# One ring of PSUM banks, late low parts on GpSimd and a new table of slots in a fused attention kernel

## The reference, cut to what matters

```python
xn = _layernorm(x)                                   # x: (8, 1024, 512), f32
out = x + attention(xn, ...) + ffn(xn, ...)

# attention: 16 heads of 64, two null keys and values for each head
a = layernorm(xn) * norm_g + norm_b
q = l2norm((a @ Wq).heads) * q_scale
k, v = split(xn @ Wkv);  k = l2norm([null_k, k]) * k_scale;  v = [null_v, v]
sim = q @ k.T * 8 + slopes[h] * -|j - i|             # ALiBi bias
sim = where(causal, sim, -max)
o = softmax(sim) @ v;  attention = o.reshape(...) @ Wout
```

## Time and profile before

| | us |
|---|---|
| median of 3 runs | 2699.43 |
| lowest, highest | 2696.95, 2702.16 |
| the profiled execution, its own time | 2701.09 |
| its span in the profile | 2699.3 |
| TensorE busy | 2627.6 (97%) |
| TensorE weight load busy | 1578.7 (58%) |
| VectorE busy | 2483.1 (92%) |
| ScalarE busy | 2127.0 (79%) |
| GpSimd busy | 2103.5 (78%) |

### The profile page before, as it was taken

How to read it: one execution, slowest core, us unless ns; L and a number is a source line. 1 busy time by engine, 2 the same in 40 slices (tenths; PEclk the granted TensorE clock), 3 DMA queues, 4 the chain that set the end, 5 groups by cost and what they waited for, 6 DMA issues and landing times.

```text
span 2699.3 us, 84329 instructions
## 1 busy us (share of the span) xinstructions
PE 2627.6 (97%) x31631; PEld 1578.7 (58%) x31631; DVE 2483.1 (92%) x6756; ACT 2127.0 (79%) x3385; POOL 2103.5 (78%) x2442
## 2 busy tenths in 40 slices
PE   5899999999999999999999999999999999999997
PEld 4456556565565565565565565566555665565654
DVE  8999998999989999999999999999999999989996
ACT  5688887888877888877888878788887888877876
POOL 6677887779867788678877788778887778877774
PEclk7899999999999999999999999999999999999999
DMA  5333354334544344433443436443453434544222
GB/s 170 74 67 72 79 105 98 89 73 82 100 100 94 69 87 97 98 85 78 96 103 82 89 75 102 102 92 72 78 106 89 101 71 78 100 102 74 57 56 71
DMA packets 638789, 236.94 MB, mean 88 GB/s; under 512 B 594608, under 2 KB 596656, under 8 KB 638384
## 3 DMA queue, kind: packets, MB, share of 16 engines
q1 hardware_dynamic: 636912, 231.45, 40.4%
q10 hardware_dynamic: 1472, 0.09, 0.0%
HBM read 72.01 MB, written 16.78 MB: 33 GB/s over the span
## 4 chain that ended last, share of the span: by engine, by line
PE 84%; DVE 7%; DMA 3%; issue 3%; POOL 2%; SPq 1%; ACT 1%; ACTq 0%; POOLq 0%; DVEq 0%
PE PS L1268 13%; PE PS L1245 12%; PE PS L1246 11%; PE PS L1247 11%; PE PS L1292 6%; PE PS L1331 6%; PE PS L1335 4%; PE PS L1333 4%; PE PS L1272 4%; PE PS L1358 4%; PE PS L1359 4%; PE PS L1360 4%; DVE PS L1044 2%; PE PS L1303 1%; DVE QKB L1064 1%
## 5 line engine op out<-in xcount | busy, mean ns | idle before, releaser
L1044 DVE CUSTOM_DVE_ANT_0 PS<-PS,STR 128x512 f32<-128x512 f32 (+3 forms) x1536 | 822.5, 580 | 124.3 <-PE PS L1292 117.4
L598 ACT ACTIVATE AR<-PS,SC 128x1024 f32<-128x1024 f32 (+1 forms) x640 | 655.0, 1023 | 146.5 <-PE PS L1303 76.8
L1245 PE MATMUL PS<-WH,XT 128*128 128x388 f16 x2048 | 677.3, 331 | 20.7 <-DVE AR L1057 10.8
L1246 PE MATMUL PS<-WL,XT 128*128 128x388 f16 x2048 | 674.6, 329 | 0.0
L1247 PE MATMUL PS<-WH,XT 128*128 128x388 f16 x2048 | 674.2, 329 | 0.0
L602 ACT ACTIVATE AR<-AR 128x1024 f16<-128x1024 f32 (+1 forms) x640 | 621.7, 971 | 20.3
L810 POOL TENSOR_TENSOR RN<-SS,HALF 128x8 f32<-128x8 f32 x256 | 453.6, 1772 | 179.2 <-DVE SS L1132 178.0
L1085 DVE TENSOR_TENSOR AR<-AR 128x768 f16<-128x768 f32 (+1 forms) x448 | 503.1, 1134 | 13.2 <-ACT AR L602 13.2
L1268 PE MATMUL PS<-AR 64*128 64x512 f16 (+3 forms) x4608 | 496.7, 324 | 9.2 <-ACT AR L598 9.2
L1331 PE MATMUL PS<-AR 128*128 128x66 f16 x4608 | 473.0, 195 | 2.1 <-DVE AR L1085 1.2
L1333 PE MATMUL PS<-AR 128*128 128x64 f16 x4608 | 469.4, 192 | 0.0
(11 more groups left out here) (227 smaller groups left out, 5199.7 us busy)
## 6 DMA issues: line engine op xcount, KB each, us to landing
XW<-in_L_attn_x SPq DMA_DIRECT2D x112, 256.0 KB, 3.1
XB<-in_L_attn_x SPq DMA_DIRECT2D x64, 256.0 KB, 2.9
out<-ACC SPq DMA_DIRECT2D x64, 256.0 KB, 2.3
ACC<-in_L_attn_x SPq DMA_DIRECT2D x56, 256.0 KB, 3.0
AR<-QKB SPq DMA_TRANSPOSE x512, 2.5
AR<-in_L_attn_Wkv SPq DMA_DIRECT2D x2, 1536.0 KB, 12.7
ACC<-in_L_attn_x SPq DMA_DIRECT2D x2, 1024.0 KB, 7.1
AR<-in_L_attn_Wout SPq DMA_DIRECT2D x1, 2048.0 KB, 8.3
```

The costliest lines, as they stand in the source:

```text
L598: e.activation(PR[:, n % 2, :, 0:wide], SB[:, :, 0:wide], ACT.Exp, scale=SIG).then_inc(s_p, 1)
L1044: e.tensor_tensor_reduce(out=r[:, 0:n], in0=r[:, 0:n], in1=ST[:, u % 2, h, o:o + n], scale=1.0, scalar=LOW, op0=ALU.add, op1=ALU.max, accu ...
L1245: e.matmul(to, XT[:, k, xs], WH[:, k, p, :], start=k == 0, stop=False)
L1246: e.matmul(to, XT[:, k, xs], WL[:, k, p, :], start=False, stop=False)
```

## The change

- **One ring of six banks** (0 to 5) now serves scores, pieces, projected and output tiles. A score step takes two adjacent banks (`take_pair`), and `bank_free` waits for the exp that read them last. AV moves to banks 6 and 7. TensorE issues pieces ahead of scores in a slot.
- **Pieces in groups**: the 12 pieces become 10 groups; (0,0) and (2,0) share a pair of banks, and so do (4,1) and (6,1). Matmuls and maxima are the same in number and size.
- **The cast** of a step (L602) has a slot of its own, `W_CAST`, and no longer follows its exp directly.
- **Late low parts** 8 to 15 are made by GpSimd in two instructions each, a scaling in place and a difference (`W_LATP`, semaphores s_spr and s_spq). The transposes of unit 1 and the projections of unit 2 wait for them.
- **The maxima** of the weights are turned in bank 5, without the wait for s_bqe; those of Wout in bank 6.
- The wait for s_nv2 ahead of the value matmuls goes (the null step stands ahead on the same engine).
- **New slots**: 50 to a unit and new offsets in all tables, of which the diff shows some.

```diff
-BANKS = 4
-SL = 48
+BANKS = 6
+SL = 50
-PIECES = [(qt, c) for qt in range(NT) for c in range(1 + qt // 4)]
+GROUPS = [[(0, 0), (2, 0)], [(3, 0)], [(1, 0)], [(4, 0)], [(5, 0)], [(4, 1), (6, 1)], [(6, 0)], [(5, 1)], [(7, 0)], [(7, 1)]]
...
-W_PIECE = [47, 53, 56, 59, 66, 68, 69, 77, 79, 82, 83, 86]
-W_MAX = [41, 45, 49, 55, 64, 64, 66, 72, 75, 75, 76, 84]
-W_SCORE = [88, 96, 105, 108, 111, 115, 118, 126, 130, 133]
-W_OTS = [109, 149]
-W_OP = [121, 121, 138, 149, 160, 160, 167, 170]
...
+W_PIECE = [56, 56, 63, 68, 78, 88, 88, 89, 92, 94]
+W_MAX = [57, 58, 62, 73, 79, 85, 85, 87, 95, 98]
+W_SCORE = [97, 98, 110, 111, 115, 115, 120, 128, 140, 141]
+W_CAST = [99, 102, 111, 111, 115, 116, 122, 129, 142, 142]
+W_OTS = [118, 155]
+W_OP = [141, 145, 145, 151, 171, 191, 194, 207]
...
-W_STAT = [-288, -194, -181, -174, -128, -113, -101, -96]
-W_XF = [-73, -53, -29, -6, -6, 11, 18, 20]
+W_STAT = [-335, -285, -235, -222, -209, -200, -167, -161]
+W_XF = [-111, -87, -60, -20, -6, 4, 12, 28]
...
-HOLD = [2.0, 2.1, 2.0, 6.7]
+HOLD = [9.6, 10.6, 11.8, 12.7, 10.3]
...
-W_LATD = [-313, -246, -231, -193, -187, -179, -171, -128, -96, -89, -73, -68, -67, 17, 19, 20]
-W_XL0 = [-78, -1]
-W_WOM = [30, 40, 41]
-W_WOT = [46, 53]
+W_LATD = [-376, -343, -342, -342, -314, -290, -252, -192]
+W_LATP = [-218, -169, -149, -144, -79, -78, -57, 48]
+W_XL0 = [0, 26]
+W_WOM = [-159, -11, 11]
+W_WOT = [25, 37]
...
+def pieces(g):
+    out, at = [], 0
+    done = 2 * sum(len(z) for z in GROUPS[:g])
+    for qt, c in GROUPS[g]:
+        n = min(512, P * (qt + 1) - 512 * c)
+        out.append((qt, c, at, n, done))
+        at += n
+        done += 2
+    return out
 
...
+    def take_pair(slot, u, m):
+        i = min(range(BANKS - 1), key=lambda z: (max(read[z], read[z + 1]), read[z] + read[z + 1]))
+        for h in range(2):
+            who = ("sc", u, 2 * m + h)
+            at[who], before[who] = i + h, last[i + h]
+            last[i + h], read[i + h] = who, slot
...
+        for u, m in due(s, W_SCORE):
+            take_pair(s + HOLD[4], u, m)
...
-        SB, AV = PS[:, 0:2, :], PS[:, 2:4, 0:264]
+        AV = PS[:, 6:8, 0:264]
...
-            return PS[:, 4 + BANK[who], :]
+            return PS[:, BANK[who], :]
...
-                e.wait_ge(s_mx, 24 * u + i + 1)
+                e.wait_ge(s_mx, 24 * u + pieces(i // 2)[-1][4] + i % 2 + 1)
+            elif what == "sc":
+                e.wait_ge(s_p, NS * u + i // 2 + 1)
...
-                        w.wait_ge(s_spl, 24)
+                        w.wait_ge(s_spq, 4)
...
+                    low = BANK["sc", u, 2 * m]
                     w.wait_ge(s_st, 2 * n + 2)
                     w.wait_ge(s_wo, 8)
                     pl_done(w, n - 2)
-                    e.activation(PR[:, n % 2, :, 0:wide], SB[:, :, 0:wide], ACT.Exp, scale=SIG).then_inc(s_p, 1)
+                    e.activation(PR[:, n % 2, :, 0:wide], PS[:, low:low + 2, 0:wide], ACT.Exp, scale=SIG).then_inc(s_p, 1)
+                for u, m in due(s, W_CAST):
+                    n = NS * u + m
+                    wide = width(m)
                     w.wait_ge(s_p, n + 1)
...
+                for _, i in due(s, W_LATP, 1, BL):
+                    src, scale, hi, lo = late(8 + i)
+                    w.wait_ge(s_wact, 12 + 8 + i + 1)
+                    e.tensor_scalar(src, src, scale, None, ALU.mult).then_inc(s_spr, 1)
+                    w.wait_ge(s_spr, i + 1)
+                    e.tensor_tensor(lo, src, hi, ALU.subtract).then_inc(s_spq, 1)
...
-                    qt, c = PIECES[i]
-                    n = min(512, P * (qt + 1) - 512 * c)
-                    o = 896 - P * qt + 512 * c
-                    w.wait_ge(s_s, 24 * u + 2 * i + 2)
-                    w.wait_ge(s_str, 2 * u + 2)
-                    if u:
-                        w.wait_ge(s_m, 3 * (2 * (u - 1) + qt // 4) + 3)
-                    for h in range(2):
-                        r = rb("s", u, 2 * i + h)
-                        e.tensor_tensor_reduce(out=r[:, 0:n], in0=r[:, 0:n], in1=ST[:, u % 2, h, o:o + n], scale=1.0, scalar=LOW,
-                                               op0=ALU.add, op1=ALU.max,
-                                               accum_out=MX[:, qt // 4, qt % 4, h, c:c + 1]).then_inc(s_mx, 1)
+                    for qt, c, at, n, done in pieces(i):
+                        o = 896 - P * qt + 512 * c
+                        w.wait_ge(s_s, 24 * u + pieces(i)[-1][4] + 2)
+                        w.wait_ge(s_str, 2 * u + 2)
+                        if u:
+                            w.wait_ge(s_m, 3 * (2 * (u - 1) + qt // 4) + 3)
+                        for h in range(2):
+                            r = rb("s", u, 2 * i + h)
+                            e.tensor_tensor_reduce(out=r[:, at:at + n], in0=r[:, at:at + n], in1=ST[:, u % 2, h, o:o + n], scale=1.0,
+                                                   scalar=LOW, op0=ALU.add, op1=ALU.max,
+                                                   accum_out=MX[:, qt // 4, qt % 4, h, c:c + 1]).then_inc(s_mx, 1)
                 for u, t in due(s, W_VL):
...
-            w.wait_ge(s_bqe, 3)
-            e.transpose(PS[0:8, 2, 192:320], AM[:, 0:8], IDF[:, :]).then_inc(s_amt, 1)
+            e.transpose(PS[0:8, 5, 0:128], AM[:, 0:8], IDF[:, :]).then_inc(s_amt, 1)
...
-                        w.wait_ge(s_spl, 28)
+                        w.wait_ge(s_spl, 20)
+                        w.wait_ge(s_spq, 8)
...
+                for _, i in due(s, W_WOT, 1, BL):
+                    if i == 0:
+                        w.wait_ge(s_wo, 1)
+                        e.transpose(PS[0:1, 6, 0:P], AM[:, 5:6], IDF[:, :]).then_inc(s_won, 1)
+                    else:
+                        w.wait_ge(s_wop, 1)
+                        e.matmul(PS[:, 6, P:P + 1], ONE[0:1, :], M8[0:1, :], start=True, stop=True).then_inc(s_won, 1)
+                for u, i in due(s, W_PIECE):
+                    bank_free(w, "s", u, 2 * i)
+                    bank_free(w, "s", u, 2 * i + 1)
+                    for qt, c, at, n, done in pieces(i):
+                        for g in range(qt // 2 + 1):
+                            w.wait_ge(s_kq[g], 32 * (u + 1))
+                        for h in range(2):
+                            hs = slice(64 * h, 64 * h + 64)
+                            e.matmul(rb("s", u, 2 * i + h)[:, at:at + n], KQ[hs, u % 2, QH, P * qt:P * qt + P],
+                                     KQ[hs, u % 2, KH, 512 * c:512 * c + n], start=not at, stop=True,
+                                     skip_group_check=True).then_inc(s_s, 1)
                 for u, m in due(s, W_SCORE):
                     qc, blocks = STEPS[m]
-                    n = NS * u + m
-                    w.wait_ge(s_p, n)
+                    low = BANK["sc", u, 2 * m]
+                    bank_free(w, "sc", u, 2 * m)
+                    bank_free(w, "sc", u, 2 * m + 1)
                     for g in range(max(2 * qc + 1, blocks[-1][0] // 2) + 1):
                         w.wait_ge(s_kq[g], 32 * (u + 1))
                     w.wait_ge(s_ct[qc], 16 * (u + 1))
...
-                                e.matmul(SB[:, h, to], KQ[hs, u % 2, a, ks], KQ[hs, u % 2, c, qs],
+                                e.matmul(PS[:, low + h, to], KQ[hs, u % 2, a, ks], KQ[hs, u % 2, c, qs],
...
-                    if blocks[0][0] == 0:
-                        w.wait_ge(s_nv2, 2 * u + qc + 1)
```

127 lines of the change are left out of this document (55 added, 72 removed).

## The result

| | before | after |
|---|---|---|
| median, us | 2699.27 (2696.95 to 2702.16, 4 runs) | 2714.62 (2714.09 to 2718.99, 4 runs) |
| ratio, 95% interval | | 1.0065 (1.0053 to 1.0077) |
| span of the profiled execution | 2699.3 | 2712.3 |

The change costs 15 us; 2689 was forecast. The 13.0 us between the two profiled spans lie as follows (before, from the first projection of units 0, 4 and 63, as in the earlier trace rows): to the first projection 47.80 and now 45.75; units 0 to 3 147.84 and now 156.96, +9.1; units 4 to 62 2393.94 and now 2398.25, +4.3; the end 109.7 and now 111.3, +1.6. So I read the start from unit 0's first projection on.

What follows compares the result with a forecast made beforehand. TensorE's own work was taken as the floor, busy 2382.89 of the middle's 2394.0 us. Switches -1.2, maxima -0.6, start +4, middle -8, end -5 sum to -10.8 from 2699.4: 2689 us, range 2674 to 2711 (8 in 10).

Steps and rivals of the forecast that it cites:

- The middle: Units 4 to 62: ring and new slots give back half of the 16.3 us lost, 8 us; bounds 0 and 16.3.
- the bunching: VectorE's layer-norm work crowding some units of the middle; claimed milder after the change, the reason for the 8 us gain.
- The double waits: Matmul with two semaphore waits behind a short null step: 0.16 us lost once a unit, stays; 0 taken, bounds 6.4 either way.
- The start: Before the steady units: VectorE idles for Wout's load, GpSimd's low parts stay hidden; 4 us lost, bounds 0 and 8.
- The end: Behind the last units: score matmuls wait less for exp, 5 of 7.8 us gained; bounds 7.8 gain, 3 loss.
- Switches and maxima bank: TensorE: 12 fewer switches between 128-row and 64-row matmuls, 1.2 us less; start: maxima in their own bank, 0.6 less.
- Rival 1: Second null step waits for VectorE to read the accumulator AV: 16 us slower than forecast, 2705 us; chance 0.18.
- Quiet unit: Sign in the middle: period of a unit without layer norm stays 40.3 us within 0.1.
- Batch boundaries: Sign in the middle: units at batch boundaries take 41.4 us at most, not 42.2.

Runs made afterwards that it cites:

- e4_ott: Changed kernel with the first transfer that transposes attention outputs (OT<-OTK) at slot 125 instead of 129 in SyncE's order; 2698.25 us.
- e6_waits: e4_ott with two more waits of TensorE, on semaphores already reached, ahead of each of 640 score steps; 2697.59 us.
- e3_both: Changed kernel with Wout's maximum back behind the first evictions and late low parts 8 to 15 on VectorE again; 2714.02 us.
- e14_start: e7_start_ott with the steps of Wout's maximum later, VectorE's first at slot 38 instead of 31; 2694.24 us.
- e7_start_ott: e5_start with the transfer OT<-OTK at slot 125; 2694.30 us.
- e13_null: e4_ott with the wait for s_nv2, the end of TensorE's own null step, put back ahead of each half's first value step; 2710.52 us.
- e5_start: Changed kernel with all orders of once-only steps from the kernel before, Wout's maximum scaled to the new unit; 2715.07 us.
- e10_wot: e7_start_ott with TensorE's steps for Wout's maximum at slots 60 and 75, VectorE's second and third and the casts behind them; 2697.69 us.
- e2_lows: Changed kernel with late low parts 8 to 15 made by VectorE again, none by GpSimd; 2713.69 us.

## Why the prediction was wrong

**The middle (-8 in the sum; +4.3 measured).** This step failed, and it decided the sign. Its argument was that the ring and the new slots "can give back" at most 16.3 us and cost nothing, so its lower bound was 0. Taken apart by `e4_ott` there are two terms: -15.9 for ring, pieces and orders, and +20.2 for the transfer of OT, which the prediction never priced. That -15.9 lies near the bound of 16.3 is luck: 9.5 of it are the waits of the next paragraph, which sat in every quiet unit and so outside the 16.3. What is left for the bunching, 6.4, is near the 8 that were taken, though one of the two reasons given was misread: of a batch's eight L938 at most five lay within 48 slots before, not six. For the transfer, the prediction had the table: W_OTT moved from 109 to 129, W_OP from 121 to 141, the same distance of 20, and W_TP of the unit two ahead stands at 125, now ahead of the transfer, with loads of x behind it in two units of eight. A moved step was counted on TensorE, VectorE and GpSimd, and not on the queue that issues its transfer.

**The double waits (0, "the 0.16 stays").** Wrong in cause. They were waits for the ring, 9.5 us in 58 units, and went. Two more waits ahead of each score step cost nothing (`e6_waits`). The clue was in the trace: a gap that is named "issue" and is the same everywhere.

**The start (+4; +9.1 for units 0 to 3, +7.1 for the time at which unit 4 begins).** Right in its first mechanism, the wait for Wout, but too small; its upper bound of 8 held for the 7.1 and not for the 9.1. VectorE idled 7.91 us (8 forecast), the first eviction came at 74.40 (77.2 forecast), unit 3's first projection at 162.1, 6.7 late and not 4. GpSimd's low parts were called hidden and weren't: seven of them took 18.8 us and stood ahead of L839. The two together are 4.2 of the 9.1 (`e3_both`), with the other once-only steps 5.3 (`e14_start`); for 3.9 the cause stays open. What the prediction did not see is that the two delays cover each other: undone one at a time they gave +3.3 and -1.9.

**The end (-5; +1.6).** The waits of score matmuls for exp fell from 7.8 to 0.9 us, 2.3 with a piece's, as the last section of the prediction asked (under 3). The gain was taken by the next wait in line: 3.3 for the transfer of OT, 3.3 for maxima, 2.6 for GpSimd's low part. The bound of 3 on the loss side held.

**Switches and maxima bank (-1.2, -0.6).** The profiles show 1284 switches before and 1274 after, near the 12 fewer that were counted, but 1180 in the middle of both. The fewer ones lie in start and end, where larger waits hide them, and no run here shows the 1.2. The 0.6 can't be told from the 2 us by which starts differ.

**Rivals.** Rival 1 named a wait of the null step for VectorE, and its time, 2705, was nearest below the result; the mechanism did not occur (0.7 us, once, in the end). The range, 2674 to 2711, ended 4 us short: it had no term for a transfer that comes late. With it, +17 to +20, it would have held the time, with a forecast of 2706 to 2709; the 6 to 9 us from there to 2714.6 are start and end.

**The signs named.** Quiet unit 40.3 within 0.1: the quietest pair gave 40.0. Batch boundaries at most 41.4: wrong, the units that end a batch took 41.3 to 45.3 and a batch's fourth unit 41.8 to 45.2, which is where the missing term showed.

## What to carry to other kernels

When a table of slots moves a step, follow its transfer too: list what stands ahead of it in the issuing queue, and what each of those waits for. A gap that is the same in every round is not yet a fixed price; look whether another engine's step ends just ahead of it. And two delays that cover each other must be undone together, or each will look innocent.

`e14_start` and `e7_start_ott`, the change with the transfer moved and the once-only steps near their old places, are faster than both kernels, by 0.14% and 0.15% over the one before (intervals up to 0.9995 and 0.9994), a gain just clear of noise.

## What was unexpected of the hardware

- Waits for semaphores that had long been reached cost TensorE nothing, even two more ahead of each of 640 score steps (2697.59 and 2698.25 us). A wait for TensorE's own last matmul, though, cost 0.22 us in each unit (`e13_null`).
- VectorE's L1098, with two inputs in SBUF, took 2.21 us in `e5_start`, where it began at 79.01, within a 2.14 us GpSimd instruction with two inputs (L914, from 78.53); it took as long at this place in `e7_start_ott` and 2.20 in `e10_wot`. In `e3_both` it took 0.68 us, with no GpSimd instruction at work. The reduction with one input, L1187, took 4.42 us, whether GpSimd was at work throughout (the changed kernel) or not at all (`e2_lows`). The Trainium skill, page "SBUF — State Buffer", section "SBUF: two separate sides", has the lock bear on a VectorE instruction in a two-port mode or with two SBUF inputs, the latter only against a GpSimd one that reads SBUF, until the one that started first is done. These runs agree in part: the two-input instruction ended 0.6 us behind GpSimd's, and the reduction wasn't held. But in `e14_start` L1098 began 0.6 us into a GpSimd instruction of 1.64 us (L839, two small inputs, 128x8) and took 0.69 us: it was not held.
- After waits of 2.46 and 2.34 us in the middle of full work the granted clock was 0.50 for the 2 us behind them; after one of 2.44 us it stayed at 1.00. Where it fell, the wait cost about 1.5 us more than its length.
